# Graph propagation on one NeuronCore: first halves in steps of four chunks, one-hots in the rows of x, the running total on GpSimd

## The reference

```python
def _propagate(all_emb, rows, cols, vals):
    acc = all_emb
    x = all_emb
    for _ in range(N_LAYERS):
        x = jax.ops.segment_sum(vals[:, None] * x[cols], rows, num_segments=N_NODES)
        acc = acc + x
    return acc / (N_LAYERS + 1)

users_emb = all_users[users] + _upsample_nearest(mm_users[users])
items_emb = all_items + _upsample_nearest(mm_items)
rating = users_emb @ items_emb.T
rating = rating + bias_user[users] + bias_item.T
return jax.nn.sigmoid(rating)
```

## Time and profile before

| | |
|---|---|
| median of 3 runs | 5386.48 us (5386.25 to 5393.11) |
| the profiled execution: its own time | 5386.6 us |
| the profiled execution: its span | 5384.8 us |
| mean granted TensorE clock | 0.860 |
| VectorE busy | 4793.2 us (89%) |
| TensorE busy | 3361.2 us (62%) |
| ScalarE busy | 2443.1 us (45%) |
| GpSimd busy | 2415.1 us (45%) |

### The profile page before, as it was taken

One profiled execution on the slowest core, in us unless ns is written; L12 is line 12 of the kernel. 1 busy time (PEld: TensorE's weight loads), 2 busy tenths in 40 slices (PEclk: granted clock), 3 DMA queues, 4 the chain that ended last, 5 costly groups with the idle time before them and its releaser, 6 DMA issues.

```text
span 5384.8 us, 195868 instructions
## 1 busy us (share of the span) xinstructions
PE 3361.2 (62%) x71235; PEld 2864.2 (53%) x71473; DVE 4793.2 (89%) x7569; ACT 2443.1 (45%) x4368; POOL 2415.1 (45%) x2161
## 2 busy tenths in 40 slices
PE   5600021111288888777678888867768888867767
PEld 4500011110277777666567777756657777766652
DVE  9989999999999999877799999967789999977778
ACT  0035555553366666500156666620046666640027
POOL 0038763330177777700067777730037777760000
PEclk9955555555699999999999999989989999989989
DMA  9960000300188778799968878889968777879999
GB/s 329 415 260 0 0 0 3 5 0 0 64 248 253 248 246 247 234 321 328 279 213 251 248 256 249 249 276 328 328 191 255 249 245 246 249 241 328 328 281 357
DMA packets 840272, 1191.20 MB, mean 221 GB/s; under 512 B 150792, under 2 KB 667583, under 8 KB 839825
## 3 DMA queue, kind: packets, MB, share of 16 engines
q1 hardware_dynamic: 716032, 816.66, 53.2%
q0 software_dynamic: 123872, 372.78, 18.0%
q10 hardware_dynamic: 304, 1.00, 0.1%
HBM read 638.35 MB, written 551.90 MB: 221 GB/s over the span
## 4 chain that ended last, share of the span: by engine, by line
DVE 28%; DMA 28%; issue 20%; POOL 9%; PE 6%; ACT 5%; SPq 1%; DVEq 1%; POOLq 0%; another core or an unknown queue 0%; ACTq 0%
DMA ring<-posts 15%; DMA posts<-ring 9%; POOL posts L775 9%; DVE store L1064 6%; PE psum L1501 4%; DVE total L861 3%; ACT new L695 3%; DVE store L1042 3%; DVE ring L1271 3%; DVE store L1043 2%; DMA out<-new 2%; DVE new L1243 2%; DVE ring L1256 2%; DVE ring L1295 2%; DMA ring<-lanes_d 1%
## 5 line engine op out<-in xcount | busy, mean ns | idle before, releaser
L775 POOL DMA_INDIRECT posts<-ring x1884 | 1852.6, 983 | 1740.6 <-DVE ring L1256 1154.0
L1477 PE MATMUL psum<-store,ring 128*128 x45216 | 2086.2, 197 | 497.9 <-DVE ring L1271 461.6
L1477 PEld LDWEIGHTS psum<-store,ring 128*128 128x128 bf16 x45216 | 1815.1, 100 | 769.2 <-issue 591.4
L695 ACT ACTIVATE new<-new 128x512 bf16<-128x512 uint8 x1884 | 1067.8, 614 | 0.0
L1271 DVE TENSOR_SCALAR ring<-ring,lane_f 128x1024 bf16<-128x1024 bf16 x1884 | 959.7, 551 | 23.4 <-DMA ring<-lanes_d 22.0
L1295 DVE TENSOR_TENSOR ring<-ring,wide_lane 128x1024 bf16<-128x1024 bf16 x948 | 612.9, 688 | 300.1 <-ACT ring L705 300.1
L1256 DVE TENSOR_TENSOR ring<-new 128x1024 bf16<-128x1024 bf16 x942 | 652.2, 692 | 93.8 <-ACT new L695 63.3
L693 ACT ACTIVATE ring<-new 128x512 bf16<-128x512 bf16 x942 | 585.9, 622 | 310.3 <-DVE new L1243 308.2
L750 POOL TENSOR_TENSOR ring<-store 128x1024 f32<-128x1024 f32 x157 | 369.6, 2354 | 660.6 <-DVE store L982 306.3
L1243 DVE TENSOR_TENSOR new<-psum,vals_m 128x512 f32<-128x512 f32 x942 | 644.1, 684 | 6.1 <-PE psum L1477 4.0
L1501 PE MATMUL psum<-ring 128*128 128x64 bf16 x11520 | 387.4, 193 | 188.7 <-DVE ring L1295 180.9
(11 more groups left out here) (228 smaller groups left out, 2666.1 us busy)
## 6 DMA issues: line engine op xcount, KB each, us to landing
ring<-lanes_d SPq DMA_DIRECT2D x471, 512.0 KB
ring<-posts SPq DMA_DIRECT2D x240, 772.0 KB, 6.7
store<-posts SPq DMA_DIRECT2D x234, 772.0 KB, 6.7
posts<-store SPq DMA_DIRECT2D x2, 30880.0 KB, 166.7
posts<-store SPq DMA_DIRECT2D x2, 30108.0 KB, 128.5
out<-new SPq DMA_DIRECT2D x96, 500.0 KB, 8.4
posts<-ring POOLq DMA_INDIRECT x1884
store<-L_rec_bias_item SPq DMA_DIRECT2D x1, 3125.0 KB, 13.8
```

What stands on the lines that cost most here:

```text
L695: last = nc.scalar.activation(digits[s][:, k, :], scaled_byte[s][k], ACT.Copy, scale=scale)
L775: pool.indirect_dma_start(out=posts[:, :], out_offset=bass.IndirectOffsetOnAxis(ap=dring[:, h, c:c + 1], axis=0), in_=msg[:, n, :], in_off ...
L1477: last = pe.matmul(psum[:, d % 4, (n % 2 * BLOCK + b) * F:(n % 2 * BLOCK + b + 1) * F], of, xflat[:, bass.ds(at_d[c] * F + (k * XT + x * F ...
```

## The change

A step of the first half now takes four chunks: the one-hots are 128x2048 each and lie in `new`, over the rows of x; `scaled` moves to `ring`; products, mask, high parts and digits double in width; PSUM takes two banks a step, four steps in turn. VectorE's instructions per four chunks go from ten to five, their columns in all stay. The 16 slots are refilled in four groups of four, each with a semaphore of its own, and GpSimd waits for `s_msg` once every four scatters; the number of scatters stays. Since the one-hots overwrite x, the first step waits for the whole splitting and for all seven takes; these are done by GpSimd, ahead of its first scatter of the layer. The rests of the splitting move from the lanes' place in `ring` to that of the messages, so that SyncE loads the first lanes of a layer during the splitting, and ScalarE waits for its end before it refills.

```diff
@@ sizes and buffers @@
-SENT_ROWS = [16 * (8 * BODIES + REST), 16 * 8 * BODIES]
-DUOS = CHUNKS // 2
+SENT_ROWS = [16 * (4 * BODIES + REST)] + 3 * [16 * 4 * BODIES]
+QUADS = CHUNKS // 4
-        hot = [ring[:, 2048 + s * 1024:3072 + s * 1024].bitcast(BF16).rearrange("p (k e) -> p k e", k=2) for s in range(2)]
+        hot = [new[:, s * WAYS * 1024:(s + 1) * WAYS * 1024].bitcast(BF16).rearrange("p (k e) -> p k e", k=WAYS) for s in range(2)]
-        scaled = [new[:, s * 512:(s + 1) * 512] for s in range(2)]
+        scaled = [ring[:, 2048 + s * 1024:3072 + s * 1024] for s in range(2)]
-        rest = [ring[:, s * SPLIT * F:(s + 1) * SPLIT * F].rearrange("p (t f) -> p t f", f=F) for s in range(2)]
+        rest = [ring[:, 5200 + s * SPLIT * F:5200 + (s + 1) * SPLIT * F].rearrange("p (t f) -> p t f", f=F) for s in range(2)]
@@ SyncE @@
-                sp.wait_ge(s_x3, (layer + 1) * SPLITS)
+                if layer:
+                    sp.wait_ge(s_unit, layer * ITERS + GOTS)
@@ ScalarE @@
-                        act.wait_ge(s_scat[h], i * 128 + layer * SENT_ROWS[h])
-                    at = bass.ds(i * 16 + h * 8, n)
+                        act.wait_ge(s_scat[h], i * 64 + layer * SENT_ROWS[h])
+                    at = bass.ds(i * 16 + h * 4, 4)
-                        nc.scalar.activation(msg_parts[:, 0, 4 * d:4 * d + 4, :], scaled_high[s], ACT.Copy).then_inc(s_high, 1)
+                        nc.scalar.activation(msg_parts[:, 0, 8 * d:8 * d + 8, :], scaled_high[s], ACT.Copy).then_inc(s_high, 1)
+                act.wait_ge(s_x3, (layer + 1) * SPLITS)
                 take_apart(0, True)
@@ GpSimd @@
+                if layer:
+                    pool.wait_ge(s_add, layer * ITERS + 2)
+                else:
+                    pool.wait_ge(s_lanesd, 64)
+                    pool.wait_ge(s_decoded, 1)
+                    pool.wait_ge(s_x0, 1)
+                for q in range(SPLITS):
+                    a, b = q * SPLIT, (q + 1) * SPLIT
+                    if layer == 0:
+                        nc.gpsimd.tensor_copy(total3[:, a:b, :], new3[:, a:b, :]).then_inc(s_taken, 1)
+                    else:
+                        nc.gpsimd.tensor_tensor(total3[:, a:b, :], total3[:, a:b, :], new3[:, a:b, :], ALU.add).then_inc(s_taken, 1)
+
                 def scatter(i, chunks):
                     for n in range(chunks):
-                        h, c = n // 8, n % 8
-                        if n % 2 == 0:
-                            pool.wait_ge(s_msg, i * 8 + (layer * DUOS + n // 2 + 1))
+                        h, c = n // 4, n % 4
+                        if c == 0:
+                            pool.wait_ge(s_msg, i * 4 + (layer * QUADS + h + 1))
@@ VectorE @@
-                def send(i, first, pairs=8):
-                    for d in range(pairs):
-                        h, j = d // 4, d % 4
-                        dve.wait_ge(s_sent, i * 8 + (layer * DUOS + d + 1))
+                def send(i, first, quads=4):
+                    for d in range(quads):
+                        h, b = d // 2, d % 2
+                        dve.wait_ge(s_sent, i * 4 + (layer * QUADS + d + 1))
                         if not (first and d < 2):
-                            if first and d == 2:
-                                dve.wait_ge(s_taken, layer * SPLITS + 2)
-                            scale(i, (d + 6) % 8, d - 2)
-                        for k in range(2):
-                            last = nc.vector.tensor_scalar(hot[d % 2][:, k, :], idx[j // 2][:, j % 2 * 2 * CHUNK:(j % 2 + 1) * 2 * CHUNK],
-                                                           lane_f[:, k:k + 1], None, ALU.is_equal)
+                            scale(i, (d + 2) % 4, d - 2)
+                        for k in range(WAYS):
+                            last = nc.vector.tensor_scalar(hot[b][:, k, :], idx[b], lane_f[:, k:k + 1], None, ALU.is_equal)
                         if not (first and d < 3):
-                            low_parts(i, (d + 5) % 8, d - 3)
-                        if first and d < SPLITS:
-                            take(layer, d)
-
+                            low_parts(i, (d + 1) % 4, d - 3)
+
+                dve.wait_ge(s_taken, (layer + 1) * SPLITS)
                 send(0, True)
```

More of the change, by code:

```diff
@@ L357, in build @@
         s_high = sem("s_high")
-        s_scat = [sem(f"s_scat{h}") for h in range(2)]
+        s_scat = [sem(f"s_scat{h}") for h in range(4)]
         s_got = [sem(f"s_got{s}") for s in range(GOTS)]
@@ L1322, in _ @@
                         add(i * 2, 1 + g, at_t[g])
-                add(ITERS // 2, -1, tiles_at(ITERS - 1, 1)[0])
+                for s in range(ADD_BODIES * GOTS + 1, ITERS - 1):
+                    prepare(0, s + 1, (s + 1) % GOTS)
+                    add(0, s, tiles_at(s, 1)[0])
+                add(0, ITERS - 1, tiles_at(ITERS - 1, 1)[0])
             dve.wait_ge(s_add, LAYERS * ITERS + 2)
```

107 lines of the change are left out of this document (49 added, 58 removed).

## The result

The changed kernel takes **5739.53 us** (median of 4 runs, 5733.85 to 5754.87) against 5387.11 us (5386.25 to 5393.11) for the kernel before: ratio 1.0656, 95% interval 1.0633 to 1.068. The profiled execution took 5733.85 us, with a span of 5731.8, 347 us more than the profiled execution before.

The account below looks back on a forecast made before the run. GpSimd's scatter DMAs, 0.96 us plus 0.30 us gaps, were taken to bound the first halves. DMA waits +355, splitting +36 and filling +18 sum to 409; 5386.6 + 409 = 5796 us, range 5430 to 5950.

Parts of the forecast that it names:

- GpSimd's DMAs set the pace, and fewer VectorE instructions save nothing: First halves: GpSimd needs 5.06 us per four chunks, VectorE at most 4.45 after the change; nothing saved by itself.
- The rival by which VectorE sets the pace: First-half body: 0.30 us gaps are waits for VectorE, four chunks fall from 5.06 to 4.45; 5154 us, chance 0.06.
- the one by which the engines stop meeting: Rival: with larger operations at new places no DMA waits, and the adds fit beside the splitting; 5352 us, chance 0.07.
- the one by which the phase is held as before: Rival: DMAs wait 0.023 us as before, one-hots and mask giving way and soaking up VectorE's slack; 5441 us, chance 0.13.
- The favourable phase goes, +355: First-half scatters: DMAs begin anywhere in VectorE's step and wait 0.211 us each, 398 us less today's 43: +355 us.
- The formula: First-half DMAs: an operation of length d in cycle T costs each DMA on average (d - 0.13)² / 2T.
- The cycle: First-half step of four chunks, waits included: T = 5.06 + 4 x 1.245 / T, so 5.90 us.
- The hold needs a VectorE without slack: First-half body: DMAs stay nearly free of waits only without VectorE slack; the change gives it 0.6 us in 5.06.
- Splitting, +36: Splitting: GpSimd's running total and VectorE's products take turns at SBUF; +15 us in layers 1 and 2, +6 in layer 0.
- Filling, +18: Start of each first half: first DMA comes 16.1 us after the first one-hot instead of 10.1; +6 three times.
- Slots refilled by four, "nothing": Slot refills: waiting for four scatters instead of eight only lets VectorE run further ahead; 0 us unless GpSimd runs dry.
- What would show it: Profile signs: mean DMA about 1.17 us, durations up to 2, 0.30 us issue gaps, first halves about 950 us, VectorE idle at refills.

Follow-up runs that it names:

- b_half_scale: The kernel before with VectorE's scaling cut to the first four of a step's eight edges; 5475.48 us, ratio 1.0188.
- pad_turns: half_turns with one useless VectorE product (1, 3, 5 edges in layers 0, 1, 2) added per step of four chunks; 5460.27 us, ratio 1.0166.
- half_turns: The changed kernel with every VectorE operation of a step in two halves, in the order of the kernel before; 5531.18 us, ratio 1.0293.
- half_product: The changed kernel with the product of the low parts alone issued in two halves; 5610.74 us, ratio 1.0298.
- half_hots: The changed kernel with the one-hots alone issued in two halves each; 5678.79 us, ratio 1.0433.
- b_slots4: The kernel before with its slots refilled in four groups of four instead of two of eight; 5306.96 us, ratio 0.9876.
- pace_scan: The changed kernel with VectorE's one-hots and product gated on GpSimd's semaphore, plus small products of 0, 1, 3 edges by layer; 5716.31 us, ratio 1.0638.

## Why the prediction was right, point by point

- **GpSimd's DMAs set the pace, and fewer VectorE instructions save nothing: right.** VectorE's busy time fell by 126 us a layer, GpSimd's gaps stayed at 0.30 us. The rival by which VectorE sets the pace (5154) is out. So are the one by which the engines stop meeting (5352) and the one by which the phase is held as before (5441).
- **The favourable phase goes, +355: right as a sum, measured +372; the working behind it only in part.** That a DMA is held by what lies beyond its first 0.13 us of a product or one-hot is what the trace shows (0.84 us behind their ends). That DMAs begin at any point of VectorE's step is not: they meet the head of the first one-hot in nearly every step. The formula's parts can be set beside the trace, by what VectorE was executing at a DMA's start. Products caught 334 DMAs, 168 us (forecast 0.605 / 5.9 x 1884 = 193); one-hots 459 DMAs, 226 us (175); masks 9.5 (29). The chance to be caught by a one-hot came out as worked (2 x 0.74 / 5.9 = 0.25, found 0.24) by luck: the formula spreads it over two one-hots, and all but 6 of the 459 were caught by the first. What a one-hot costs a DMA that it catches was 0.49 us, not 0.37, because the DMA begins 0.13 us into it and has nearly all of it ahead; the second one-hot adds nothing here, since these DMAs end 0.84 us behind the end of the first. Errors of both signs, +51, -25 and -20 us, are what left the sum close. The cycle, 4 x (1.181 + 0.305) = 5.94 us, was forecast as 5.90.
- **"The hold needs a VectorE without slack": open.** b_half_scale and pad_turns go the way of it: with more slack the waits rise, with less they fall. But both edits also move the one-hots against the product, and half_turns, with the slack of the kernel before, has 214 us of waits where that has 44. half_product and half_hots show that the length of the operations matters too, in part by moving where the next DMA begins. The prediction treated the loss of the phase as one switch and the length only as its price. What decides the phase in which the two engines settle, no run shows.
- **Splitting, +36: measured +30.** Layer 0's copies on GpSimd took 18.00 us for seven, 2.57 each, inside its 0 to 2.89, but cost only 2.7 us of splitting where +6 was put; layers 1 and 2 +14 each for +15. The alternation read from the earlier trace rows is what the trace shows, with adds and products above 3 us as announced, and here the rule of the Trainium skill ("SBUF — State Buffer", section "Who interferes with whom") agrees too: each engine is held for a whole instruction of the other.
- **Filling, +18: measured +16.** The first DMA comes 16.0 us after the first one-hot, forecast 16.1.
- **Slots refilled by four, "nothing": wrong, the one term that was missing.** It is worth -64 us by itself (b_slots4), by the pauses. The rows were there: the earlier trace rows put 1731 gaps at 586.5 us, 0.339 each, while 0.30 stood in the steady stretch; 1731 x 0.305 = 528 leaves 58 us of "issue" that the sum of 833 us a layer passed over ("of the other 39 us some 14 are DMAs that took longer"), and the remaining 25 a layer were never asked after. This is more than the whole 56 us by which the forecast was too high; the other terms, +17, -6 and -2 us off, together took 9 back.
- **What would show it:** mean DMA 1.17 us (1.181), durations up to 2 (2.03), gaps of 0.30 put down to issue (1881 of 1884), VectorE idle at refills (546.7 us at the product behind ScalarE): all seen. None of these signs tells DMAs that begin anywhere from DMAs in a bad fixed phase. The first halves, announced at about 950 us, took 922 to 946, lower by the pauses.

## What to carry to other kernels

When two engines share a path and the one that isn't the bound is made faster, ask what held the two in step: a little slack that is soaked up by giving way may be what keeps them apart, and less work on the faster one can cost more than it saves. Before a mean over all phases is used, look where in the other engine's operations the starts fall: a hold at one place sets where the next start falls, and a sum that agrees does not show that the starts are spread. Ask of every "issue" gap whether its mean is that of the steady stretch; the difference times the count is a term of its own. And take a change of many parts apart on the chip: here two of its parts gain 1.6%, and beside them the rest loses 8%.

## What was not expected of the hardware

- A DMA that a product holds up leads the next one into the head of the first one-hot (316 of 330 in the changed kernel), so one wait brings the next.
- Work added to VectorE made the kernel faster (5531.18 to 5460.27 us, ratios 1.0293 and 1.0166), and work taken away made it slower (b_half_scale, 1.0188).
- GpSimd paused for some 4.5 us every 112 indirect DMAs while eight slots shared a semaphore, and not with four; the cause is open.
- A semaphore increment placed ahead of an indirect DMA on GpSimd was counted before that DMA, and some before the DMA ahead of it, began (the fourth by 3.7 us in pace_scan's layer 0; VectorE, gated on it, was up to 12 chunks ahead, where 6 were allowed), and it took no time of its own (0.30 us between DMAs with and without it).
- A one-hot of twice the columns takes less than twice the time: 745 ns in the changed kernel against 551 before, with the DMAs' interference in both.
